# Two attention sublayers of a decoder: one ring of three PSUM bank pairs, exponentials of two heads at a time, and small operations moved from VectorE to GpSimd

## The chip, the cores and the metric

The kernel runs on one core of a Trainium2 chip. The metric is the time of one execution in microseconds (us); several runs are made and the median is taken. A core has five engines, each with its own queue of instructions that it executes in order: TensorE (PE in the rows, its weight loads PEld), VectorE (DVE), ScalarE (ACT), GpSimd (POOL) and SyncE (SP, which issues transfers). They wait for one another through semaphores. TensorE and the others exchange results in PSUM, which has eight banks of 512 float32 columns on 128 partitions; everything else lies in SBUF. TensorE runs at 2.4 GHz or, when the chip grants less, at 1.2 GHz; the granted clock is given as a share of full speed.

## The reference

A decoder of four layers works on x of shape (4, 512, 128). Each of its twelve sublayers computes `x = layernorm(x + f(x))`. Two of them are self attentions with 16 heads of 8 dimensions, and only they are changed:

```python
# layer 1: l1a
q = q * scale                              # q, k, v: (4, 16, 512, 8)
attn = softmax(einsum('bhnd,bmhd->bhnm', q, k))
return einsum('bhnm,bmhd->bnhd', attn, v) @ w_proj.T + b_proj

# layer 3: l3a
attn = where(causal, einsum('bhqd,bhkd->bhqk', q, k) * scale, -inf)
a = clip(attn, -100, 100)
e = exp(a - max(a))
p = e / (sum(e) + 1e-6) + 1e-8
return einsum('bhqk,bhkd->bhqd', p / sum(p), v) @ w_proj.T
```

## The kernel before

`attention16` builds both sublayers, l1a with the full table and l3a with the causal one. The work is cut into 16 groups m = 0 to 15: four batches of four groups of four heads. What is done to a group is cut into units, and a unit has a part on each of several engines:

- J: projections of one batch. Queries and keys are split into three bf16 parts, high (ScalarE), the remainder "left" (VectorE, L674), middle (ScalarE) and low (VectorE, L679), and written to DRAM; SyncE gathers them per group into QS and KS, so that one bf16 matmul gives a float32 score. J 5 copies the values into Va (L685). In l3a VectorE then adds two sums of values, Vsum (L689, L691).
- A: scores of one query tile for two heads, two matmuls into a pair of banks (L515), and the row maxima on VectorE (L701).
- P: the maxima of a group are split into three bf16 parts by four small VectorE operations (L713 to L719), in l3a after a clip (L709).
- T: eight matmuls transpose these parts into a bank pair (L523), and VectorE adds them to QS (L724), so that the next score matmul has the maximum subtracted.
- B: transposed scores of one key tile for one head (L543) and the exponential on ScalarE, 512 columns (L640). In l3a the columns shrink from 512 to 128 with the key tile, and L is the exponential of the lower clip bound (L540, L633).
- X (l3a alone): the clip of one key tile's exponentials of four heads, on VectorE (L729), `e = max(min(e, 1), LB)`, 2048 to 512 columns.
- V: the value matmuls of one or two key tiles (L570, and L567 for the rows under the causal mask), into bank 6; after the last ScalarE copies the bank (L645).
- F: transposes of that copy (L576) and the division by the sum on VectorE (L748 and L750; in l3a L739 to L750).
- C, W, Y, N: once a batch, concatenation, output projection, norm statistics, norm apply and transposes.

What sets the order is a table per sublayer, CAUSAL and FULL, with CAUSAL_BATCH and FULL_BATCH for what is put in once a batch. The tables name units relative to the current group; every engine walks the same list and executes its part of each unit, in order. An engine that waits therefore holds up all that stands behind it in its own queue.

PSUM before: A and T share two bank pairs (banks 0 to 3), B and L two single banks (4 and 5), V has bank 6, the rest bank 7. GpSimd has little to do here: it clears KS and Mp at the start and computes the reciprocal deviation of the norms.

Of the kernel before, what the change touches and what calls it, by code (L numbers as in the profile page):

```python
# [366 lines left out]
def attention16(k, name, w, causal=False):  # L367
# [38 lines left out]
    place = lambda m, kt: HG * ((m * NT + kt) % sets)  # L406

    def body(block, projected, high_made, rest_made, middle_made, low_made, zeroed, v_taken, pair_ready, pair_free, max_split, s_ready, exp_done,
             clipped, pv_done, o_copied, o_turned, ctx_done, c_turned, c_taken, out_ready, steps, normed, turned, v_summed, xt_made,
# [9 lines left out]
        E = k.sb(name + "E", [P, sets * HG, S])  # L419
# [36 lines left out]
        def _(pe):
# [24 lines left out]
            for u in order:  # L481
                kind, m = u[0], u[1]
                g = m % G
                if u in ut:
# [21 lines left out]
                elif kind == "A":  # L506
                    _, _, qt, hp = u
                    if ut[u] == 0:
                        pe.wait_ge(zeroed, 2)
# [15 lines left out]
                elif kind in "BL":  # L525
                    _, _, kt, j = u
                    n = ub[u]
                    if n == 0:
                        for at in (4, 5, 6):
                            if at in users:  # L530
                                emptied(users[at])
                    if n >= 2:
                        pe.wait_ge(exp_done, n - 1)
                    if kt == 0 and j == 0:
                        pe.wait_ge(pair_free, ut[("T", m)] + 1)
                    o = PS[:, 4 + n % 2, :]
                    pp, par = 2 * g + j // 2, j % 2
                    q0 = kt * P if causal else 0
                    if kind == "L":
                        ins = mm(o, k.maxrows[:, par, :], QS[:, pp, :], start=True, stop=True)  # L540
                    else:
                        o = o[:, q0:S]
# [3091 lines left out]
```

## Time and profile before

| | us |
|---|---|
| median of 3 runs | 2062.26 (2058.0 to 2062.41) |
| profiled execution | 2065.93 |
| its span | 2063.8 |
| VectorE busy in the span | 1394.2 |
| TensorE busy | 1671.3 |
| ScalarE busy | 1009.2 |
| GpSimd busy | 414.3 |

The span is the time between the first and the last instruction; the rest of the profiled execution lies around it. Busy sums over the whole span say little here, since twelve sublayers with different limits follow one another. The sublayer l1a lies from about 285 us to 562 us, l3a from 1463 us to 1792 us. Within them the T units (L724, one a group) mark the groups: the distance between two of them is the time of a group. Consecutive VectorE instructions overlap by some 0.08 us in the records, so the cost of one in a row of several is the distance between two starts.

### The profile page before, as it was taken

What the parts mean: (1) busy time and instruction counts of PE and PEld (TensorE: products, weight loads), DVE (VectorE), ACT (ScalarE), POOL (GpSimd) and SP (SyncE); (2) the same over time, 40 slices, a digit from 0 to 9 for tenths busy, and PEclk for the clock granted to TensorE, in tenths of its full rate; (3) what the DMA queues carried; (4) which work ended last, traced back from release to release, by engine and by line L of the source; (5) the groups of instructions that cost most, each with busy time, mean ns of one, the idle gap of its engine ahead of it and who ended that gap; (6) DMA issues with size and microseconds to landing.
All of it is one profiled execution on the core that took longest, in us unless ns stands there. A gap on an engine that the chain in (4) does not pass through costs nothing. (4 is left out here: it accounts for less than half of the span.)

```text
span 2063.8 us, 32418 instructions
## 1 busy us (share of the span) xinstructions
PE 1671.3 (81%) x11422; PEld 990.5 (48%) x11422; DVE 1394.2 (68%) x3239; ACT 1009.2 (49%) x2161; POOL 414.3 (20%) x575
## 2 busy tenths in 40 slices
PE   5779859999878999957789999973587878798692
PEld 3546533333365666645544444531344444365582
DVE  4646678888584777765566767767788889665434
ACT  3336536666523554535355555542245545465362
POOL 1110030000034666541200000001200000100375
PEclk9989869999989999987799999995688999999797
DMA  4100021221046888850000000000211110000213
GB/s 116 41 1 2 1 71 61 63 62 31 1 165 256 333 326 328 324 180 1 1 1 1 1 1 1 1 1 18 71 56 58 32 58 16 1 2 14 94 53 84
DMA packets 71545, 151.09 MB, mean 73 GB/s; under 512 B 9042, under 2 KB 55419, under 8 KB 66299
## 3 DMA queue, kind: packets, MB, share of 16 engines
q1 hardware_dynamic: 61211, 136.25, 19.0%
q0 software_dynamic: 4992, 10.23, 1.6%
q10 hardware_dynamic: 5184, 2.55, 0.5%
q8 instruction: 93, 1.52, 0.3%
q14 instruction: 65, 0.53, 0.1%
HBM read 124.46 MB, written 29.26 MB: 74 GB/s over the span
## 5 line engine op out<-in xcount | busy, mean ns | idle before, releaser
L162 POOL TENSOR_SCALAR rstd<-MV 128x2 f32<-128x2 f32 (+1 forms) x100 | 25.9, 259 | 999.7 <-DVE MV L130 995.0
L640 ACT ACTIVATE l1aE<-PS 128x512 f32<-128x512 f32 x256 | 142.2, 596 | 75.5 <-PE PS L543 72.9
L701 DVE TENSOR_REDUCE l1aM<-PS 128x2 f32<-128x1024 f32 x128 | 150.4, 1218 | 26.2 <-PE PS L515 24.6
L640 ACT ACTIVATE l3aE<-PS 128x512 f32<-128x512 f32 (+3 forms) x256 | 102.7, 439 | 111.7 <-PE PS L545 108.8
L2582 ACT COPY PT<-PS 128x512 f32<-128x512 f32 x128 | 69.2, 589 | 93.5 <-PE PS L2493 93.2
L701 DVE TENSOR_REDUCE l3aM<-PS 128x2 f32<-128x256 f32 (+3 forms) x128 | 100.2, 817 | 15.7 <-PE PS L517 15.5
L2672 DVE TENSOR_REDUCE M<-PS 128x1 f32<-128x589 f32 x128 | 92.5, 764 | 27.0 <-PE PS L2482 26.7
L1713 PE MATMUL PS<-WB,H 128*128 128x512 f32 x234 | 107.4, 595 | 0.0
L2588 ACT ACTIVATE E<-PS,M 128x589 f32<-128x589 f32 x128 | 95.9, 763 | 17.6 <-DVE M L2672 17.5
L543 PE MATMUL PS<-l1aQS,l1aKS 128*128 128x512 bf16 x256 | 90.6, 388 | 8.5 <-ACT l1aE L640 7.0
L729 DVE SCALAR_TENSOR_TENSOR l3aE<-l3aE,l3aLB 128x2048 f32<-128x2048 f32 (+1 forms) x64 | 94.9, 1482 | 2.7 <-ACT l3aE L640 2.7
L515 PE MATMUL PS<-l1aKS,l1aQS 128*128 128x512 bf16 x256 | 82.2, 406 | 16.0 <-DMA l1aKS<-head_image 9.4
L1853 ACT ACTIVATE H<-PS,WB 128x128 f32<-128x128 f32 x156 | 44.6, 368 | 90.8 <-PE PS L1701 90.7
L543 PE MATMUL PS<-l3aQS,l3aKS 128*128 128x512 bf16 (+3 forms) x256 | 76.7, 322 | 10.3 <-ACT l3aE L640 9.7
L2510 PE MATMUL PS<-PT,Va 128*64 128x512 f32 x320 | 82.8, 616 | 0.8 <-ACT Q L2593 0.8
L2493 PEld LDWEIGHTS PS<-cols_const_sb,E 128*128 128x128 f32 x512 | 58.2, 144 | 49.6 <-DVE E L2692 29.4
L515 PE MATMUL PS<-l3aKS,l3aQS 128*128 128x128 bf16 (+3 forms) x256 | 66.9, 316 | 15.1 <-DVE l3aM L701 8.9
L164 POOL TENSOR_TENSOR rstd<-rstd,mhalf 128x2 f32<-128x2 f32 (+1 forms) x100 | 75.9, 759 | 8.3
L2482 PE MATMUL PS<-K,Q 64*128 64x512 f32 x256 | 75.1, 664 | 0.0
L1866 ACT ACTIVATE A<-PS,WB 128x128 f32<-128x128 f32 x156 | 58.7, 457 | 32.4 <-PE PS L1723 32.4
L2493 PE MATMUL PS<-cols_const_sb,E 128*128 128x128 f32 x512 | 71.4, 283 | 2.8 <-DVE E L2692 2.6
L2692 DVE TENSOR_SCALAR E<-E,sums 128x589 f32<-128x589 f32 x128 | 67.6, 528 | 4.5
(671 smaller groups left out, 4273.1 us busy)
## 6 DMA issues: line engine op xcount, KB each, us to landing
WB<-in_experts SPq DMA_DIRECT2D x39, 1286.0 KB
TB<-mixed_tails SPq DMA_DIRECT2D x39, 768.5 KB, 7.1
l1aQS<-head_image SPq DMA_DIRECT2D x16, 256.0 KB, 2.9
l1aKS<-head_image SPq DMA_DIRECT2D x32, 128.0 KB, 3.0
l3aQS<-head_image SPq DMA_DIRECT2D x16, 256.0 KB, 2.9
l3aKS<-head_image SPq DMA_DIRECT2D x32, 128.0 KB, 3.1
head_image<-l1aparts SPq DMA_DIRECT2D x8, 384.0 KB, 2.5
head_image<-l3aparts SPq DMA_DIRECT2D x8, 384.0 KB, 2.5
```

Of the source, the lines that this page charges most:

```text
L164: g.tensor_tensor(out, out, self.mhalf[:, 0:out.shape[1]], ALU.pow).then_inc(done, 1)
L515: ins = mm(o, QS[:, pp, qt * P:(qt + 1) * P], KS[:, pp, par, 0:kc], start=True, stop=not causal)
L543: ins = mm(o, KS[:, pp, par, kt * P:(kt + 1) * P], QS[:, pp, q0:S], start=True, stop=not causal)
L640: nc.scalar.activation(E[:, place(m, kt) + j, q0:S], PS[:, 4 + n % 2, q0:S], ACT.Exp, scale=SCALE).then_inc(exp_done, 1)
L701: v.tensor_reduce(M[:, m % 2, qt, 2 * hp:2 * hp + 2], PS[:, bank:bank + 2, 0:kc], AX, ALU.max, negate=True).then_inc(pair_free, 1)
L729: v.scalar_tensor_tensor(e, e, 1.0, LB[:, m % 2, :, kt * P:S], ALU.min, ALU.max).then_inc(clipped, 1)
L1713: mm(o, H1[:, i % 3, c * P:(c + 1) * P], mid_w(i, c), start=False, stop=False)
L2482: ins = mm(PS[:, at_ + 2 * par, :], Q[own, b % 2, pp, q], K[own, b % 2, pp, :], start=True, stop=True)
L2493: ins = nc.tensor.transpose(PS[:, at_ + 2 * par, t * P:(t + 1) * P], E[:, ring(x, par), e0:e0 + P], k.ident)
L2510: ins = mm(PS[64 * par:64 * par + 64, 6, :], Va[:, b % 2, t, h * DH:(h + 1) * DH], PT[:, n % 2, par, t, :], start=(t == 0), stop=(t == len ...
L2588: nc.scalar.activation(E[:, i, 0:NK], scores(s, par), ACT.Exp, bias=M[:, i:i + 1], accum_out=sums[:, i:i + 1]).then_inc(exp_done, 1)
L2672: ins = v.tensor_reduce(M[:, i:i + 1], scores(s, par), AX, ALU.max, negate=True)
```

## The change

There is now one ring of three bank pairs (banks 0 to 5) through which A, T, B and L go in the order of the table: unit i has pair i modulo 3 and waits until the unit three places ahead has been read. B and L take two heads, so that one exponential reads 1024 columns of two banks. E holds five key tiles instead of three. V is one unit of all four key tiles of a group. In l1a KS has no padded half: each score matmul reads 64 rows, the two heads of a pair in the two row halves, and KS is gathered by one transfer instead of two.

On GpSimd now: P, the low parts of the queries and keys of batches 1 to 3, and the Vsum additions of l3a. The clearing of Va moves from VectorE's start to just ahead of the first value copy. GpSimd walks the table too, the norm operations included.

```diff
-    ('B', 0, 2, 1), ('B', 0, 2, 2), ('V', 0, 0, 1), ('B', 0, 2, 3), ('X', 0, 1), ('B', 0, 3, 0), ('T', 1), ('X', 0, 2), ('B', 0, 3, 1),
+    ('B', 0, 0, 1), ('A', 1, 1, 1), ('B', 0, 1, 1), ('B', 0, 1, 0), ('X', 0, 0), ('A', 2, 0, 0), ('B', 0, 3, 1), ('X', 0, 1), ('P', 1),
+    ('B', 0, 2, 1), ('B', 0, 3, 0), ('B', 0, 2, 0), ('X', 0, 3), ('X', 0, 2), ('T', 1), ('A', 2, 0, 1), ('V', 0, 0, 4),
...
+    ('B', -1, 3, 1), ('T', 0), ('V', -1, 0, 4), ('A', 1, 0, 0), ('B', 0, 1, 0), ('A', 1, 2, 1), ('B', 0, 1, 1), ('A', 1, 1, 1),
...
+    SLOTS, SETS = 3, 5
+    rows_of = lambda par: slice(0, P) if causal else slice(64 * par, 64 * par + 64)
...
+    pairs = [u for u in order if u[0] in "ABLT"]
+    slot_of = {u: i % SLOTS for i, u in enumerate(pairs)}
...
-                    n = ut[u]
-                    bank = 2 * (n % 2)
+                    bank = 2 * slot_of[u]
...
-                        ins = mm(o, QS[:, pp, qt * P:(qt + 1) * P], KS[:, pp, par, 0:kc], start=True, stop=not causal)
+                        own = rows_of(par)
+                        key = KS[:, pp, par, :] if causal else KS[own, pp, :]
+                        ins = mm(o, QS[own, pp, qt * P:(qt + 1) * P], key[:, 0:kc], start=True, stop=not causal)
...
+                elif kind == "P":
+                    pool.wait_ge(pair_free, ut[last_a[m]] + 1)
...
+                    if causal:
+                        step(g.tensor_scalar(Mg, Mg, -LIM, LIM, ALU.max, ALU.min))
+                        step.wait()
+                    maxima, rest = (a.rearrange("p t (a r) -> p a t r", a=2) for a in (Mg, Mleft[:, :, :]))
+                    high, middle, low = (Mp[:, :, :, DK * i + AUG_SLOT:P:64] for i in range(3))
+                    step(g.tensor_copy(high, maxima))
+                    step.wait()
+                    step(g.tensor_tensor(rest, maxima, high, ALU.subtract))
+                    step.wait()
+                    step(g.tensor_copy(middle, rest))
+                    step.wait()
+                    g.tensor_tensor(low, rest, middle, ALU.subtract).then_inc(max_split, 1)
...
-                        nc.scalar.activation(E[:, place(m, kt) + j, q0:S], PS[:, 4 + n % 2, q0:S], ACT.Exp, scale=SCALE).then_inc(exp_done, 1)
+                        q0, at = kt * P if causal else 0, place(m, kt) + 2 * hp
+                        nc.scalar.activation(E[:, at:at + 2, q0:S], PS[:, bank:bank + 2, q0:S], ACT.Exp, scale=SCALE).then_inc(exp_done, 1)
```

The order on TensorE in a plain group of l1a, around the value unit (L570, now L583), before:

```order
L515 MATMUL PS<-l1aKS,l1aQS 128x512 x2
L543 MATMUL PS<-l1aQS,l1aKS 128x512
L570 MATMUL PS<-l1aE,l1aVa 32x512 x8
L515 MATMUL PS<-l1aKS,l1aQS 128x512 x2
L543 MATMUL PS<-l1aQS,l1aKS 128x512 x2
L576 MATMUL PS<-cols_const_sb,l1aOs 128x128 x4
L523 MATMUL PS<-ident_b,l1aMp 128x128 x8
```

and after (L538 is T, L530 A, L554 B):

```order
L538 MATMUL PS<-ident_b,l1aMp 128x128 x8
L583 MATMUL PS<-l1aE,l1aVa 32x512 x16
L530 MATMUL PS<-l1aKS,l1aQS 128x512 x2
L554 MATMUL PS<-l1aQS,l1aKS 128x512 x2
L530 MATMUL PS<-l1aKS,l1aQS 128x512 x2
```

The value work of a group stood in two halves between score matmuls; now it is one block directly behind T's transposes, and the next pair of scores for a maximum stands behind the block.

The order on VectorE in a plain group of l3a, from the clip of the first key tile to T, before:

```order
L701 TENSOR_REDUCE l3aM<-PS 128x2 x3
L729 SCALAR_TENSOR_TENSOR l3aE<-l3aE,l3aLB 128x2048
L709 TENSOR_SCALAR l3aM<-l3aM 128x16
L713 CAST l3aMp<-l3aM 128x16
L715 TENSOR_TENSOR l3aMleft<-l3aM,l3aMp 128x2x4x2
L717 CAST l3aMp<-l3aMleft 128x16
L719 TENSOR_TENSOR l3aMp<-l3aMleft,l3aMp 128x16
L729 SCALAR_TENSOR_TENSOR l3aE<-l3aE,l3aLB 128x4x384
L724 TENSOR_TENSOR l3aQS<-PS,l3aQS 128x1024
```

and after (L745 the maxima, L757 X, L751 T):

```order
L745 TENSOR_REDUCE l3aM<-PS 128x2 x4
L757 SCALAR_TENSOR_TENSOR l3aE<-l3aE,l3aLB 128x2048
L745 TENSOR_REDUCE l3aM<-PS 128x2
L757 SCALAR_TENSOR_TENSOR l3aE<-l3aE,l3aLB 128x4x384
L757 SCALAR_TENSOR_TENSOR l3aE<-l3aE,l3aLB 128x4x128
L757 SCALAR_TENSOR_TENSOR l3aE<-l3aE,l3aLB 128x4x256
L751 TENSOR_TENSOR l3aQS<-PS,l3aQS 128x1024
```

The five splitting operations are gone from VectorE's queue, and all four clips stand ahead of T. The five now stand on GpSimd, whose queue in a plain group of l3a holds only them:

```order
L643 TENSOR_SCALAR l3aM<-l3aM 128x16
L647 CAST l3aMp<-l3aM 128x16
L649 TENSOR_TENSOR l3aMleft<-l3aM,l3aMp 128x2x4x2
L651 CAST l3aMp<-l3aMleft 128x16
L653 TENSOR_TENSOR l3aMp<-l3aMleft,l3aMp 128x16
```

Each of them waits for the one ahead of it, the first for the last maximum of the group. On TensorE in the same group, from T to the next maximum's scores, before:

```order
L570 MATMUL PS<-l3aE,l3aVa 32x512 x4
L543 MATMUL PS<-l3aQS,l3aKS 128x256
L545 MATMUL PS<-causalT_b,ident_b 128x128
L543 MATMUL PS<-l3aQS,l3aKS 128x128
L545 MATMUL PS<-causalT_b,ident_b 128x128
L523 MATMUL PS<-ident_b,l3aMp 128x128 x8
```

and after:

```order
L530 MATMUL PS<-l3aKS,l3aQS 128x128
L532 MATMUL PS<-causal_b,ident_b 128x128
L530 MATMUL PS<-l3aKS,l3aQS 128x128
L532 MATMUL PS<-causal_b,ident_b 128x128
L583 MATMUL PS<-l3aE,l3aVa 32x512 x4
L580 MATMUL PS<-l3aLB,l3aVsum 32x128 x8
L580 MATMUL PS<-l3aLB,l3aVa 32x128 x4
L583 MATMUL PS<-l3aE,l3aVa 32x384 x4
L583 MATMUL PS<-l3aE,l3aVa 32x256 x4
L583 MATMUL PS<-l3aE,l3aVa 32x128 x4
L530 MATMUL PS<-l3aKS,l3aQS 128x384
```

The first value tile stood ahead of T's transposes; now the whole value unit stands behind T and one pair of scores, and the next scores for VectorE behind it.

## Rows read from the trace of the kernel before

**Rows 1.** Stretches: us, busy us of PE, PEld, DVE, ACT, POOL, PEclk, DMA.

```profile
300.00:317.00 17.00, 12.53 (x32) 2.81 (x32) 14.55 (x16) 1.57 (x3) 0.00 (x0) 0.50 0.19 61
1488.00:1764.00 276.00, 226.51 (x2081) 124.44 (x2081) 240.11 (x399) 147.95 (x329) 3.69 (x8) 0.90 0.13 41
```

**Rows 2.** Timeline, VectorE, one group of l3a: start, us, engine, line, [idle before <-releaser].

```profile
1715.28 1.22 DVE L724 TENSOR_TENSOR l3aQS<-PS,l3aQS 128x1024 bf16<-128x1024 f32 x1
...
1719.07 0.42 DVE L701 TENSOR_REDUCE l3aM<-PS 128x2 f32<-128x256 f32 x1 [0.50 <-PE PS L517]
...
1725.91 2.28 DVE L729 SCALAR_TENSOR_TENSOR l3aE<-l3aE,l3aLB 128x2048 f32<-128x2048 f32 x1
1728.11 0.17 DVE L709 TENSOR_SCALAR l3aM<-l3aM 128x16 f32<-128x16 f32 x1
...
1729.11 1.75 DVE L729 SCALAR_TENSOR_TENSOR l3aE<-l3aE,l3aLB 128x1536 f32<-128x1536 f32 x1
1731.94 1.23 DVE L724 TENSOR_TENSOR l3aQS<-PS,l3aQS 128x1024 bf16<-128x1024 f32 x1 [1.08 <-PE PS L523]
```

**Rows 3.** Groups by form, l3a: count | busy us, mean ns | idle before.

```profile
L701 DVE TENSOR_REDUCE l3aM<-PS 128x2 f32<-128x256 f32 x32 | 13.4, 420 | 12.5 <-PE PS L517 12.5
```

**Rows 4.** Timeline, l1a: T units, one wait of VectorE, one value unit.

```profile
311.31 1.23 DVE L724 TENSOR_TENSOR l1aQS<-PS,l1aQS 128x1024 bf16<-128x1024 f32 x1 [1.26 <-PE PS L523]
...
375.49 2.50 DVE L701 TENSOR_REDUCE l1aM<-PS 128x2 f32<-128x1024 f32 x2 [1.48 <-PE PS L515]
...
482.19 1.92 PE L570 MATMUL PS<-l1aE,l1aVa 128*32 128x512 f32 x16
...
507.80 1.22 DVE L724 TENSOR_TENSOR l1aQS<-PS,l1aQS 128x1024 bf16<-128x1024 f32 x1
...
521.33 1.22 DVE L724 TENSOR_TENSOR l1aQS<-PS,l1aQS 128x1024 bf16<-128x1024 f32 x1
...
534.45 1.23 DVE L724 TENSOR_TENSOR l1aQS<-PS,l1aQS 128x1024 bf16<-128x1024 f32 x1
```

**Rows 5.** Timeline, TensorE, l3a: transposes of T, first value tile, lower-bound matmuls.

```profile
1652.89 0.61 PE L523 MATMUL PS<-ident_b,l3aMp 128*128 128x128 bf16 x8
...
1728.44 1.94 PE L570 MATMUL PS<-l3aE,l3aVa 128*32 128x512 f32 x8 [1.27 <-DVE l3aE L729]
...
1730.82 1.01 PE L523 MATMUL PS<-ident_b,l3aMp 128*128 128x128 bf16 x8
...
1731.99 0.65 PE L567 MATMUL PS<-l3aLB,l3aVsum 128*32 128x128 f32 x16
```

**Rows 6.** Groups by form: the maxima of l1a, exponentials of 512 and 1024 columns.

```profile
L701 DVE TENSOR_REDUCE l1aM<-PS 128x2 f32<-128x1024 f32 x128 | 150.4, 1218 | 26.2 <-PE PS L515 24.6
L640 ACT ACTIVATE l1aE<-PS 128x512 f32<-128x512 f32 x256 | 142.2, 596 | 75.5 <-PE PS L543 72.9
L2265 ACT ACTIVATE E<-E 128x1024 f32<-128x1024 f32 x8 | 8.5, 1060 | 10.8 <-DVE E L2301 10.6
```

**Rows 7.** Timeline, VectorE and GpSimd together at three places.

```profile
927.25 1.13 DVE L2065 SCALAR_TENSOR_TENSOR R<-WB,pair_w,R 128x128 f32<-128x128 f32 x4
927.43 0.24 POOL L162 TENSOR_SCALAR rstd<-MV 128x2 f32<-128x2 f32 x1
...
930.75 1.13 DVE L2065 SCALAR_TENSOR_TENSOR R<-WB,pair_w,R 128x128 f32<-128x128 f32 x4
930.90 1.05 POOL L162 TENSOR_SCALAR rstd<-MV 128x2 f32<-128x2 f32 x1
...
1768.28 0.66 DVE L729 SCALAR_TENSOR_TENSOR l3aE<-l3aE,l3aLB 128x512 f32<-128x512 f32 x1
1768.45 0.56 POOL L162 TENSOR_SCALAR rstd<-MV 128x2 f32<-128x2 f32 x1
```

**Rows 8.** Groups by form, GpSimd: count | busy us, mean ns | idle before.

```profile
L1782 POOL TENSOR_TENSOR rs<-rs,mhalf 128x1 f32<-128x1 f32 x78 | 44.0, 564 | 6.5
L2845 POOL TENSOR_TENSOR R<-R,YB 128x512 f32<-128x512 f32 x3 | 3.8, 1256 | 9.1 <-ACT YB L2906 9.1
```

More of the change, by code:

```diff
@@ L390, in attention16 @@
     ut, ub = (count([u for u in order if u[0] in kinds]) for kinds in ("AT", "BL"))
+    pairs = [u for u in order if u[0] in "ABLT"]
+    slot_of = {u: i % SLOTS for i, u in enumerate(pairs)}
+    slot_prev = {u: pairs[i - SLOTS] for i, u in enumerate(pairs) if i >= SLOTS}
     uj = count([u for u in order if u[0] == "J" and u[2] not in (2, 4)])
-    pairs = list(ut)
+    first = lambda kinds: {m: next(u for u in pairs if u[0] in kinds and u[1] == m) for m in range(NG)}
+    first_a, first_b = first("A"), first("BL")
     last_a = {u[1]: u for u in ut if u[0] == "A"}
+    last_b = {u[1]: i for u, i in ub.items() if u[0] == "B"}
+    last_exp = {u[1:3]: i + 1 for u, i in ub.items() if u[0] == "B"}
+    last_low = {u[1]: i + 1 for u, i in ub.items() if u[0] == "L"}
     singles = [u for u in order if u in uj or u[0] in "FCWN"]
-    ring = (7, 4, 5, 6)
+    ring = (7, 6, 5, 4)
     bank_of, bank_prev, users = {}, {}, {}
@@ L418, in body @@
         Mp = k.sb(name + "Mp", [P, 2, NT, P], BF16)
[L419 removed]
+        E = k.sb(name + "E", [P, SETS * HG, S])
         Os = k.sb(name + "Os", [P, 2, S])
@@ L525, in _ @@
                 elif kind in "BL":
[L526 to L542, printed above, removed]
-                        ins = mm(o, KS[:, pp, par, kt * P:(kt + 1) * P], QS[:, pp, q0:S], start=True, stop=not causal)
-                        if causal:
-                            ins = mm(o[:, 0:P], k.ident_b, k.causalT_b, start=False, stop=True)
+                    hp = u[-1]
+                    if u == first_b[m]:
+                        pe.wait_ge(pair_free, ut["T", m] + 1)
+                    pp = 2 * g + hp
+                    for par in range(2):
+                        o = PS[:, bank + par, :]
+                        if kind == "L":
+                            ins = mm(o, k.maxrows[:, par, :], QS[:, pp, :], start=True, stop=True)
+                        else:
+                            kt = u[2]
+                            q0 = kt * P if causal else 0
+                            own = rows_of(par)
+                            key = KS[:, pp, par, :] if causal else KS[own, pp, :]
+                            ins = mm(o[:, q0:S], key[:, kt * P:(kt + 1) * P], QS[own, pp, q0:S], start=True, stop=not causal)
+                            if causal:
+                                ins = mm(o[:, q0:q0 + P], k.ident_b, k.causalT_b, start=False, stop=True)
                     ins.then_inc(s_ready, 1)
@@ L602, in _ @@
             g = nc.gpsimd
-            g.memset(KS[P // 2:P, :, 0, :], 0.0).then_inc(zeroed, 1)
-            pool.wait_ge(zeroed, 1)
-            g.memset(KS[0:P // 2, :, 1, :], 0.0).then_inc(zeroed, 1)
-            pool.wait_ge(zeroed, 2)
             g.memset(Mp[:, :, :, :], 0.0).then_inc(zeroed, 1)
-            for b in range(BT):
-                k.norm_gpsimd(pool, b, b)
+            if causal:
+                pool.wait_ge(zeroed, 1)
+                g.memset(KS[P // 2:P, :, 0, :], 0.0).then_inc(zeroed, 1)
+                pool.wait_ge(zeroed, 2)
+                g.memset(KS[0:P // 2, :, 1, :], 0.0).then_inc(zeroed, 1)
@@ L660, in _ @@
             step = Count(dve, steps)
-            step(v.memset(Va[:, :, :, :, :], 0.0))
-            step.wait()
-            step(v.memset(Va[:, :, :, :, AUG:AUG + 1], 1.0))
             for u in order:
@@ L698, in _ @@
                     dve.wait_ge(pair_ready, ut[u] + 1)
-                    bank = 2 * (ut[u] % 2)
+                    bank = 2 * slot_of[u]
+                    if u == first_a[m] and m >= 2:
+                        dve.wait_ge(max_split, m - 1)
                     kc = (qt + 1) * P if causal else S
@@ L732, in _ @@
                     dve.wait_ge(o_turned, m + 1)
+                    if causal and g == 0:
+                        dve.wait_ge(v_summed, b + 1)
                     turned_o = PS[:, bank_of[u], :].rearrange("p (t j d) -> p t j d", t=NT, j=HG)
```

127 lines of the change are left out of this document (66 added, 61 removed), and 18 rows, old and new, of tables (CAUSAL, CAUSAL_BATCH, FULL, FULL_BATCH).

## The prediction

> **What bounds the kernel now.** The change touches two of twelve sublayers, the full attention l1a and the causal attention l3a, so I read those stretches alone. First the table by stretch [rows 1]: from the first T unit of l3a to the last, 276 us, VectorE is busy 240.1 of 276, ScalarE 148, GpSimd 3.7, and the granted clock is 0.90. VectorE sets the pace there. Then the timeline of VectorE over one plain causal group [rows 2], T to T: 16.66 us. In it VectorE waits twice, 0.50 us for a score pair and 1.08 us for T's transposes, and works the rest. Its five splitting operations (P, L709 to L719) fill 1.00 us, from 1728.11 to 1729.11. The grouped row behind [rows 3] says the same of all groups: the maxima of 256 columns wait 12.5 us in total for TensorE.
>
> In l1a sixteen T units start between 311.31 and 534.45, 223.1 us, and a plain group takes 13.53 [rows 4]. VectorE has one long wait per group there, 1.48 us behind the value and transpose work.
>
> **The change, full attention.** P leaves VectorE: about 0.95 us of work less per group. But the value unit is now one, of four key tiles, straight behind T on TensorE, and the next maximum stands behind both. A unit of two tiles took 1.92 us [rows 4], that is 0.86 a tile and 0.2 of run-in and end; four take 3.45. The cycle that closes on itself is then: transposes 0.6 [rows 5], values 3.45, change of tile form 0.15 (an estimate), a score pair 0.42, seven maxima of 1.2 [rows 6] less 0.04 overlap each, one F of 0.5 (estimate from its two operations), 0.2 for the B pair ahead of T: 13.5 to 13.6. So P's microsecond returns as a wait for V, about 2.4 where 1.48 was. ScalarE, now eight exponentials of 1024 columns, has 8 x 1.06 + 0.6 = 9.1 us [rows 6] of 13.6 and stays behind that; sixteen of 512 cost 9.5. Score matmuls on 64 rows each: 512 columns at 2.4 GHz are 0.21 us, so a pair costs 0.21 if the two row halves run side by side and 0.42 if not (estimates); only one pair a group is on the path. Projections of the next batch no longer stop VectorE as they do (low parts on GpSimd, spread over two groups): about 2.7 us a batch back, 8 in all. Against that stands the clock. With half the score columns, TensorE is lightly used between V and the next T; at the head, where scores alone run beside maxima, it was granted 0.50 for 17 us [rows 1]. I charge 0.5 us a group, 8 in all: nothing left. Head (the 3.5 us memset of Va no longer stands ahead of the first projections) -0.8, tail (eight exponentials, none of them waiting for a single bank) -2. **Full: -3**, from -12 (no clock loss) to +25 (below).
>
> **The change, causal attention.** Without P the 16.66 us group leaves 16.66 - 1.58 - 1.00 = 14.08 of VectorE work. If nothing new waited, the group would take 14.3 to 14.8, and the stage would gain over 30 us. What speaks against this is where P now runs. Its five operations depend on one another, all read SBUF, and they start when the last maximum, A(1,1,1), is done. At that moment VectorE starts X(0,0), then one short maximum, then X(0,1), X(0,3), X(0,2), then T, which needs P. X is a scalar_tensor_tensor with both operands in SBUF.
>
> The trace shows what such an instruction does to a small GpSimd operation [rows 7]. At 1768.28 an X of 512 columns starts; the 0.24 us operation that GpSimd starts at 1768.45 takes 0.56 and ends 0.07 us behind that X. At 930.75 four two-operand VectorE instructions run back to back until 931.88; the GpSimd operation begun at 930.90 takes 1.05 and ends at 931.95, again 0.07 behind the last of them: it was not let in between. In the four that start at 927.25 one did slip in (0.24 at 927.43). So P's first operation is held by X(0,0) until its end; the second fits beside the short maximum; the other three come when the row of X is over. The Trainium skill, "SBUF — State Buffer", section "Who interferes with whom", has the rule: a VectorE instruction with two SBUF inputs and a GpSimd instruction that reads SBUF exclude each other, and whichever issues first holds the shared port for its whole length. By these rows the trace agrees on the exclusion. Read instruction by instruction the rule would let GpSimd in at each border between two X, so that one operation instead of three is left at the end; the sum would then be 10 us lower than mine. The row at 930.90 is the nearer one, and I keep three.
>
> The price, with time 0 at the end of X(0,2). P ends at 0.07 + 2 x (0.08 + 0.25) = 0.73. A GpSimd operation on 128x16 is not in the trace; 0.25 lies by the 0.24 of rows 7, the other bound is the 0.56 of rows 8, which would add 0.9 a group. Hand-over 0.1. T's transposes 0.61 at full clock, 1.01 at half [rows 5]. So VectorE waits 1.44 for T, or 1.84; before it was 1.08. Behind T on TensorE's queue stand A(2,0,1) (0.25) and the whole value unit, 0.86 x (1 + 0.75 + 0.5 + 0.25) = 2.15 and 0.65 for the lower-bound matmuls [rows 5], then the score pair that VectorE needs next (0.45): 3.5 us. VectorE has 1.14 (T) + 0.34 (maximum of 256) to do: it waits 2.0. Before, V lay in four units between the X operations, so this is new. Sum: 14.08 + 1.44 + 2.0 = **17.5 at full clock.**
>
> The clock: while P is held, TensorE has nothing to do for nearly 4 us. Before, 1.27 us without work behind a light stretch (the idle time in the row at 1728.44, [rows 5]) was enough that the first value tile took 1.94 us, twice 0.86 and some, and T 1.01. In the new order T (+0.40), A(2,0,1) (+0.25) and the first value tile (+1.08) come just then: +1.7, so 19.2 in a group where the level falls. I take 19.0.
>
> Fifteen groups of 19.0 are 285. Per batch, beyond that: one q/k remainder 0.75, value copy 0.69 and its 0.29 on VectorE, projections and the concat transposes on TensorE about 1.1, norm apply 1.1, about 4; the norm statistics fall into the wait for V. Three batches: 12. First to last T: 297 for 276, **+21**. The low parts (1.26 us each on GpSimd [rows 8]) and the value sums run beside maxima of other groups, which read PSUM, and nobody waits for them. Head -0.5; tail (the last X waited for exponentials of single heads) -3. **Causal: +17.5.**
>
> The profiled execution took 2065.93, 3.7 above the median of the runs. 2065.9 - 3 + 17.5 = 2080.4 there, 2077 as a median.
>
> **Rivals.** (A) *P is ready in time.* If X does not hold these operations, or GpSimd gets in ahead of X(0,0), P ends 1.7 us after A(1,1,1) and VectorE reaches T 6 us after it. Then TensorE does T and half of V below the X, the wait for V is 0.3 to 0.7, a group takes 14.8 and a batch 7 extra: 222 + 20 = 242 for 276, -34. With head, tail and the full stage: **2022**. For it: the load row of [rows 2]. Against: every row of [rows 7]. It decides from the point at which three of P's five operations are through before X(0,1) starts. Chance 0.20.
> (B) *P is held but the clock stays up*, or GpSimd gets in at borders: 17.5 x 15 + 12 = 274.5, -1.5; total -8, **2054**. For it: T at 1652.89 ran in 0.61 [rows 5]. Chance 0.17.
> (C) *The full stage pays too.* Its A/B stretch leaves TensorE at half speed until well into V: T +0.3, pair +0.2, half of V's 3.45 doubled +1.7 = 2.2 a group, 33 in all, 25 more than I charge: **2102** with the causal loss. For it: 0.50 at the head [rows 1]. Against: V and F lie in between and keep TensorE busy. Chance 0.10.
> (D) *The full stage gains.* If the three-pair ring lets scores run far enough ahead that V is covered, a group takes VectorE's work, 11.1 to 12: -1.7 x 15 = -25, **2052** with the causal loss. Against: the first maximum behind V stands behind it in TensorE's queue. Chance 0.08.
>
> **How the numbers follow.** The forecast (P held, clock down in most groups, 2066 to 2095) has 0.45; (A) to (D) 0.20, 0.17, 0.10, 0.08. A measurement of this kernel can tell about 0.2%, 4 us, from no change. Faster than 2058: A, D, most of B: 0.38. Within: the rest of B, the low end of the forecast: 0.09. Slower than 2066: 0.53. Of the range, 2030 at the low end leaves out part of A (0.12) and 2098 most of C (0.07).
>
> **What will show it.** Right: in l3a GpSimd operations of P that take 0.5 to 2 us instead of 0.25 and end together with an X; VectorE idle 1.4 to 1.9 before T and about 2 before the first maximum behind V; T starts 18 to 20 us apart; T's eight matmuls at 1.0. In l1a T starts 13.5 to 14.2 apart with one wait of about 2.4, P on GpSimd at its plain price (no VectorE instruction there has two SBUF operands). Wrong: P's five operations in l3a end within 2 us of the last maximum, T starts 14.5 to 15 apart: then A. Wrong in the full stage: a granted clock under 0.9 there, or no wait behind V.

## The result, and the profile after

The changed kernel takes 2076.43 us (median of 20 runs, 2065.05 to 2086.04), the kernel before 2060.97 (20 runs, 2056.34 to 2066.46): 1.007 times as long, 95% interval 1.0058 to 1.0082. The forecast was 2077 within 2030 to 2098, and slower. The profiled execution has a span of 2076.0 us.

Where the time went is read from the two sublayers apart. From its first projection to the start of the next sublayer (its first matmul behind l1a, its first VectorE instruction behind l3a), l1a takes 268.1 us instead of 277.1, l3a 351.0 instead of 331.8; the rest of the difference between the two spans, 2.0 us, lies outside both. So a gain of 9.0 stands against a loss of 19.2.

The stretches of the changed kernel from the first T to the last, l1a and l3a (columns as in [rows 1]):

```profile
312.00:530.00 218.00, 178.03 (x1206) 61.28 (x1208) 178.76 (x215) 139.34 (x153) 27.97 (x78) 0.91 0.16 52
1478.00:1774.00 296.00, 225.62 (x2063) 131.92 (x2077) 223.80 (x319) 129.81 (x181) 103.31 (x95) 0.87 0.12 38
```

The second row answers to the second of [rows 1]. VectorE has 16.3 us less to do (240.1 before, 223.8 now): P's five operations were 15.0 us there and the low parts and the value sums 8.2, and some of it comes back as X that last longer and as X and F that moved into the stretch. But it stands idle for 72 us where it stood for 36. GpSimd is busy for 103 us where it was for 4. The groups by form say which waits these are and who is busy:

```profile
L745 DVE TENSOR_REDUCE l3aM<-PS 128x2 f32<-128x768 f32 x32 | 30.4, 951 | 46.0 <-PE PS L532 46.0
L751 DVE TENSOR_TENSOR l3aQS<-PS,l3aQS 128x1024 bf16<-128x1024 f32 x16 | 19.5, 1221 | 23.7 <-PE PS L538 23.7
L643 POOL TENSOR_SCALAR l3aM<-l3aM 128x16 f32<-128x16 f32 x16 | 31.9, 1997 | 150.6 <-DVE l3aM L745 150.6
...
L647 POOL CAST l3aMp<-l3aM 128x16 bf16<-128x16 f32 x16 | 13.0, 815 | 1.1
L649 POOL TENSOR_TENSOR l3aMleft<-l3aM,l3aMp 128x16 f32<-128x16 f32 x16 | 19.0, 1189 | 1.4
L651 POOL CAST l3aMp<-l3aMleft 128x16 bf16<-128x16 f32 x16 | 7.0, 435 | 1.0
L653 POOL TENSOR_TENSOR l3aMp<-l3aMleft,l3aMp 128x16 bf16<-128x16 f32 x16 | 9.1, 571 | 1.3
```

The first maximum behind the value block waits 46.0 us in all, T 23.7 (2.8 of it ahead of the first group). The five GpSimd operations of P take 2.00, 0.82, 1.19, 0.44 and 0.57 us on the mean. The same four without the clip take 0.26, 0.24, 0.25 and 0.27 in l1a (L647 to L653). One group of l3a, VectorE and GpSimd, shows why:

```profile
1604.88 2.28 DVE L757 SCALAR_TENSOR_TENSOR l3aE<-l3aE,l3aLB 128x2048 f32<-128x2048 f32 x1
1607.08 0.41 DVE L745 TENSOR_REDUCE l3aM<-PS 128x2 f32<-128x256 f32 x1
1607.41 3.52 DVE L757 SCALAR_TENSOR_TENSOR l3aE<-l3aE,l3aLB 128x1536 f32<-128x1536 f32 x3
1612.33 1.22 DVE L751 TENSOR_TENSOR l3aQS<-PS,l3aQS 128x1024 bf16<-128x1024 f32 x1 [1.39 <-PE PS L538]
...
1605.05 2.23 POOL L643 TENSOR_SCALAR l3aM<-l3aM 128x16 f32<-128x16 f32 x1 [12.63 <-DVE l3aM L745]
1607.35 0.26 POOL L647 CAST l3aMp<-l3aM 128x16 bf16<-128x16 f32 x1
1607.69 1.57 POOL L649 TENSOR_TENSOR l3aMleft<-l3aM,l3aMp 128x16 f32<-128x16 f32 x1
1609.32 0.59 POOL L651 CAST l3aMp<-l3aMleft 128x16 bf16<-128x16 f32 x1
1609.99 1.07 POOL L653 TENSOR_TENSOR l3aMp<-l3aMleft,l3aMp 128x16 bf16<-128x16 f32 x1
```

The clip of P starts 0.17 us after X(0,0) and ends at 1607.28, 0.12 behind it. The next operation falls beside the maximum, which reads PSUM, and takes 0.26. The other three each last until one of the three X in the row at 1607.41 is over; the last ends at 1611.06, 0.13 behind the end of that row. TensorE, at half clock (granted 0.50) after 2.9 us without work, does T from 1611.21 in 1.01 us:

```profile
1608.06 0.22 PE L556 MATMUL PS<-causalT_b,ident_b 128*128 128x128 bf16 x1
1611.21 1.01 PE L538 MATMUL PS<-ident_b,l3aMp 128*128 128x128 bf16 x8 [2.93 <-POOL l3aMp L653]
```

Not every group goes this way. In six of the fifteen behind the first T, P ends 0.13 us behind the last X and T waits 1.40, as here. In two, the second operation does not get in at either border between the three X, takes 3.65 us, and leaves three operations for the time behind the X; T then waits 2.37:

```profile
1627.90 3.48 DVE L757 SCALAR_TENSOR_TENSOR l3aE<-l3aE,l3aLB 128x1536 f32<-128x1536 f32 x3
1633.75 1.22 DVE L751 TENSOR_TENSOR l3aQS<-PS,l3aQS 128x1024 bf16<-128x1024 f32 x1 [2.37 <-PE PS L538]
...
1627.85 3.65 POOL L647 CAST l3aMp<-l3aM 128x16 bf16<-128x16 f32 x1
```

In three groups a value sum on GpSimd, held by X(0,0), delays P's first operation (T waits 2.04); in three a projection's VectorE instruction stands between the X and P is done before the last of them (no wait); the last group, whose A(2,0,0) is missing, waits 1.73. The last plain group of all shows the two waits and the first value tile:

```profile
1755.46 1.22 DVE L751 TENSOR_TENSOR l3aQS<-PS,l3aQS 128x1024 bf16<-128x1024 f32 x1 [1.40 <-PE PS L538]
1760.12 1.56 DVE L745 TENSOR_REDUCE l3aM<-PS 128x2 f32<-128x768 f32 x2 [3.10 <-PE PS L532]
...
1755.71 1.88 PE L583 MATMUL PS<-l3aE,l3aVa 128*32 128x512 f32 x8
```

### The profile page after: what moved, and what is told of

Read it like the earlier page. It is cut to its first block and busy times, and to the rows that moved or that the text cites. A ratio compares the mean times of both kernels' runs of the same rounds, so it can differ in the third digit from the quotient of the medians.

```text
span 2076.0 us, 32345 instructions
## 1 busy us (share of the span) xinstructions
PE 1635.2 (79%) x11384; PEld 986.3 (48%) x11422; DVE 1354.6 (65%) x3075; ACT 974.9 (47%) x1873; POOL 534.3 (26%) x737
## 3 DMA queue, kind: packets, MB, share of 16 engines
q1 hardware_dynamic: 60955, 136.25, 18.6%
## 5 line engine op out<-in xcount | busy, mean ns | idle before, releaser
L745 DVE TENSOR_REDUCE l1aM<-PS 128x2 f32<-128x1024 f32 x128 | 148.6, 1217 | 34.3 <-PE PS L530 34.1
L162 POOL TENSOR_SCALAR rstd<-MV 128x2 f32<-128x2 f32 (+1 forms) x100 | 25.6, 256 | 502.3 <-DVE MV L130 498.1
L687 ACT ACTIVATE l1aE<-PS 128x1024 f32<-128x1024 f32 x128 | 129.0, 1026 | 21.5 <-PE PS L554 16.8
L745 DVE TENSOR_REDUCE l3aM<-PS 128x2 f32<-128x256 f32 (+3 forms) x128 | 99.5, 815 | 47.4 <-PE PS L532 47.1
L687 ACT ACTIVATE l3aE<-PS 128x1024 f32<-128x1024 f32 (+3 forms) x128 | 84.8, 708 | 36.1 <-PE PS L556 34.0
L757 DVE SCALAR_TENSOR_TENSOR l3aE<-l3aE,l3aLB 128x2048 f32<-128x2048 f32 (+1 forms) x64 | 95.0, 1519 | 1.0 <-ACT l3aE L687 1.0
L554 PE MATMUL PS<-l1aQS,l1aKS 64*128 64x512 bf16 x256 | 54.2, 423 | 38.1 <-DVE l1aM L745 33.0
L554 PE MATMUL PS<-l3aQS,l3aKS 128*128 128x128 bf16 (+2 forms) x255 | 60.2, 303 | 19.0 <-DVE l3aM L745 12.5
L530 PE MATMUL PS<-l3aKS,l3aQS 128*128 128x384 bf16 (+3 forms) x255 | 67.1, 319 | 8.6 <-DVE l3aM L745 6.9
L643 POOL TENSOR_SCALAR l3aM<-l3aM 128x16 f32<-128x16 f32 x16 | 31.9, 1997 | 150.6 <-DVE l3aM L745 150.6
```

The costliest lines, as they stand in the source:

```text
L554: ins = mm(o[:, q0:S], key[:, kt * P:(kt + 1) * P], QS[own, pp, q0:S], start=True, stop=not causal)
L687: nc.scalar.activation(E[:, at:at + 2, q0:S], PS[:, bank:bank + 2, q0:S], ACT.Exp, scale=SCALE).then_inc(exp_done, 1)
L745: v.tensor_reduce(M[:, m % 2, qt, 2 * hp:2 * hp + 2], PS[:, bank:bank + 2, 0:kc], AX, ALU.max, negate=True).then_inc(pair_free, 1)
L757: v.scalar_tensor_tensor(e, e, 1.0, LB[:, m % 2, :, kt * P:S], ALU.min, ALU.max).then_inc(clipped, 1)
```

## The experiments

Each kernel is the changed one with the edit that is named. The table has what all their traces give: us from the first projection of a sublayer to the next sublayer, and between its first and last T. Each ratio is to runs of the kernel before that were made beside it (medians 2057.6 to 2062.3), with its 95% interval.

| kernel | time | ratio to before | l1a | l3a | l3a, T to T |
|---|---|---|---|---|---|
| before | 2061 | | 277.1 | 331.8 | 276.0 |
| changed | 2076.4 | 1.007 (1.006 to 1.008) | 268.1 | 351.0 | 295.9 |
| e1, X with one operand | 2006.4 | 0.976 (0.971 to 0.980) | 267.4 | 284.0 | 232.0 |
| e2, P on VectorE behind X(0,1) | 2054.1 | 0.998 (0.996 to 1.001) | 267.4 | 333.9 | 280.0 |
| e3, l3a as before | 2051.5 | 0.997 (0.994 to 0.999) | 267.9 | 327.9 | 272.2 |
| e4, all X behind T | 2032.5 | 0.989 (0.984 to 0.993) | 267.8 | 311.6 | 252.8 |
| e5, P on VectorE ahead of X(0,0) | 2042.9 | 0.989 (0.985 to 0.994) | 268.3 | 320.0 | 268.3 |
| e6, values behind three maxima | 2084.6 | 1.012 (1.009 to 1.015) | 268.1 | 357.2 | 302.2 |
| e7, l1a with P on VectorE | 2089.7 | 1.016 (1.011 to 1.020) | 284.1 | 351.1 | 296.1 |
| e8, l1a with padded keys | 2071.7 | 1.006 (1.004 to 1.009) | 270.7 | 347.3 | 292.1 |
| e9, P ahead of the X on GpSimd | 2031.5 | 0.986 (0.985 to 0.988) | 267.3 | 310.2 | 258.9 |
| e10, the same, shorter gap | 2032.2 | 0.985 (0.981 to 0.989) | 268.1 | 306.3 | 255.1 |
| e11, e9 with units respaced | 2027.1 | 0.985 (0.981 to 0.989) | 269.6 | 304.5 | 253.6 |

Stage lengths come from one execution each; the same l3a before stands at 331.8 in one and at 327.9 in e3's, so differences of 4 us say little.

**e1: the second SBUF operand of X taken away.**

```diff
-                    v.scalar_tensor_tensor(e, e, 1.0, LB[:, m % 2, :, kt * P:S], ALU.min, ALU.max).then_inc(clipped, 1)
+                    v.tensor_reduce(e, e.unsqueeze(3), AX, ALU.max).then_inc(clipped, 1)
```

> The changed kernel with one edit in the causal sublayer: X reads one SBUF operand instead of two (a maximum over an axis of length one, in place, over the same elements). The clip itself is left out, its place, length and waits stay. Theory HOLD (two-operand X instructions hold P's five operations on GpSimd): P's operations in l3a fall from 2.0, 0.8, 1.2, 0.4, 0.6 us to about 0.25 each as in l1a, the wait of 1.4 us before T goes, TensorE does T and half of V below the X, T starts 14.5 to 15.5 apart; first to last T 296 -> 240 to 255, the kernel 2076 -> about 2030. Theory ORDER (the value unit in one block behind T, with TensorE at half clock, costs this whatever P does): P short, but T starts still 18 or more apart, the kernel within 8 us of 2076.

Measured: 2006.4 us, l3a 67 us shorter. X kept its length, P lost its waits, and so did VectorE:

```profile
L757 DVE TENSOR_REDUCE l3aE<-l3aE 128x2048 f32<-128x2048 f32 x16 | 36.4, 2273 | 1.0 <-ACT l3aE L687 1.0
L643 POOL TENSOR_SCALAR l3aM<-l3aM 128x16 f32<-128x16 f32 x16 | 4.2, 265 | 140.6 <-DVE l3aM L745 140.6
L745 DVE TENSOR_REDUCE l3aM<-PS 128x2 f32<-128x768 f32 x32 | 30.3, 949 | 9.9 <-PE PS L532 9.3
...
1471.00:1704.00 233.00, 201.58 (x2113) 121.33 (x2130) 219.43 (x320) 129.87 (x181) 37.51 (x95) 0.98 0.16 49
```

The X of 2048 columns takes 2.27 us for 2.28, the clip of P 0.27 for 2.00, and the wait behind the block falls from 46.0 to 9.9 us. The last row is the stretch from first to last T: the granted clock is 0.98 where it was 0.87, so in l3a the half clock was a consequence of the late P, not a cause of its own. The order of all units is that of the changed kernel, which settles HOLD against ORDER. The gain was larger than expected (T to T 232 for 240 to 255; the kernel 2006 for about 2030). The edit frees the value sums and the low parts on GpSimd as well, so not every microsecond of it need be P's.

**e2 and e5: P on VectorE, late and early.**

```diff
+P_VECTOR = lambda causal: causal
...
-                elif kind == "P":
+                elif kind == "P" and not P_VECTOR(causal):
...
+                elif kind == "P" and P_VECTOR(causal):
...
```

The second cut is in GpSimd's part, the third in VectorE's, where the same five operations follow.

> The changed kernel with one edit in the causal sublayer: the five operations of P go back to VectorE, at the place that P has in the new table (between X(0,1) and X(0,3)). HOLD: VectorE has 1.0 us more work a group, no wait before T; T starts 15.3 to 16 apart, first to last T 296 -> 250 to 260, the kernel about 2033. ORDER: T starts 18 or more apart, the kernel 2068 or more.

Measured: 2054.1, between the two. The wait before T is gone, but not the one behind the block. This is one plain group of e2: P's last operation, the two X behind it, T, and the first three maxima, the last two in one row:

```profile
1733.88 0.23 DVE L768 TENSOR_TENSOR l3aMp<-l3aMleft,l3aMp 128x16 bf16<-128x16 f32 x1
1733.98 1.82 DVE L779 SCALAR_TENSOR_TENSOR l3aE<-l3aE,l3aLB 128x512 f32<-128x512 f32 x2
1735.72 1.21 DVE L773 TENSOR_TENSOR l3aQS<-PS,l3aQS 128x1024 bf16<-128x1024 f32 x1
1736.85 0.41 DVE L748 TENSOR_REDUCE l3aM<-PS 128x2 f32<-128x256 f32 x1
1740.23 1.55 DVE L748 TENSOR_REDUCE l3aM<-PS 128x2 f32<-128x768 f32 x2 [2.97 <-PE PS L535]
```

P ends at 1734.1, 5.3 us behind the start of the clips (X(0,0) at 1728.79), because its place in the table is behind X(0,1). I had overlooked that the engine is not all: P is late there on VectorE too, T and the block start late, and the block costs its 3 us. e5 moves P ahead of X(0,0).

```diff
-    ('B', 0, 0, 1), ('A', 1, 1, 1), ('B', 0, 1, 1), ('B', 0, 1, 0), ('X', 0, 0), ('A', 2, 0, 0), ('B', 0, 3, 1), ('X', 0, 1), ('P', 1),
+    ('B', 0, 0, 1), ('A', 1, 1, 1), ('P', 1), ('B', 0, 1, 1), ('B', 0, 1, 0), ('X', 0, 0), ('A', 2, 0, 0), ('B', 0, 3, 1), ('X', 0, 1),
```

> As the run with P on VectorE in the causal sublayer, but P stands directly behind the last maximum, ahead of X(0,0), instead of behind X(0,1). That run lost the wait before T (1.3 us in all) but kept a wait of 3 us behind the value block, since P still ended late and T and the block with it. LATE (what costs is that P ends late, on whichever engine): here P ends 1 us behind the last maximum, TensorE does T and half of the block below the X, the wait behind the block falls from 36 us in all to under 12; T starts 15.0 to 16.2 apart, first to last T 296 -> 242 to 258, the kernel 2018 to 2036. BLOCK (the one value unit costs its 3 us wherever P ends): the kernel 2048 to 2058 as with P behind X(0,1).

Measured: 2042.9. The wait behind the block falls from 36.1 us in all to 19.0, more than LATE's bound of 12, and the time lies between the two ranges. What is left of the wait is seen on TensorE. P ends at 1708.98 there, but T stands in TensorE's queue behind score pairs that wait 1.60 us for a bank, which the maximum behind X(0,0) frees. T then ran at 1712.09, 2.7 us ahead of VectorE's T, and yet the first value tile met the half clock:

```profile
1711.53 0.23 PE L557 MATMUL PS<-l3aQS,l3aKS 128*128 128x128 bf16 x1 [1.60 <-DVE l3aM L748]
...
1712.09 0.66 PE L541 MATMUL PS<-ident_b,l3aMp 128*128 128x128 bf16 x8
...
1713.11 1.94 PE L586 MATMUL PS<-l3aE,l3aVa 128*32 128x512 f32 x8
1714.82 1.08 PE L583 MATMUL PS<-l3aLB,l3aVsum 128*32 128x128 f32 x16
```

Only one other group has so long a first tile (1.94); T itself took about 1.06 in five. Why e1, in nearly the same order, stays close to full clock is not shown. Against e1, VectorE has 21 us more work from first to last T here (240.55 in 269 us for 219.43 in 233) and 15 us more idle time. The work is P's: 15 us, and 6 more because in three groups its clip and its first copy, 0.17 and 0.20 us elsewhere, took 1.1 to 1.2 while GpSimd worked on the low parts or a value sum. So ending P early is one part of the matter and VectorE's saved microsecond another; of the kernels tried, those with P on GpSimd and no hold have both.

**e6: the value block moved away from T.** `('V', -1, 0, 4)` stands behind the first three score pairs of the next group, and F behind it; P stays under the X. The two L units move as well: they stood between those score pairs and now stand behind the block.

> P stays on GpSimd under the X as in the changed kernel; only the value unit of the causal sublayer moves, behind the first three score pairs of the next group, and F with it. This prices the second part of the loss alone. P's operations stay long and the wait before T stays at 1.0 to 1.4 us; the wait behind the block (47 us in all) falls to under 20. First to last T 296 -> 258 to 275, the kernel 2040 to 2058. If the wait behind the block is not what the late P costs, under 8 us change.

Measured: 2084.6, a miss. The wait did not shrink; it moved from the second maximum behind T to the fifth:

```profile
1721.02 1.23 DVE L751 TENSOR_TENSOR l3aQS<-PS,l3aQS 128x1024 bf16<-128x1024 f32 x1 [2.37 <-PE PS L538]
1722.16 3.09 DVE L745 TENSOR_REDUCE l3aM<-PS 128x2 f32<-128x256 f32 x4
1728.48 1.23 DVE L745 TENSOR_REDUCE l3aM<-PS 128x2 f32<-128x1024 f32 x1 [3.23 <-PE PS L532]
```

The block then starts at 1723.91 instead of right behind T, and the maxima that stand ahead of it were to cover it with 3.1 us of work that the late T had also delayed; the two L units now lie between the block and the next pair, 0.9 us more. Taken alone, a change of 8 us in the wrong direction speaks rather for the second reading that was named. It is e1 that ties the wait to the late P; e6 shows that moving the block alone does not buy it back.

**e3, e7, e8: the full sublayer.** e3 builds l1a with the changed function and l3a with the function of before.

> The change in the full sublayer alone: l1a as changed, l3a as before. By the two traces l1a takes 268.1 instead of 277.1 from its first projection to the next sublayer, so the kernel should take 2061 - 9 = 2052 (2046 to 2057), both theories alike. If it takes 2061 or more, the nine microseconds were no gain of that sublayer.

Measured: 2051.5, as expected, with l1a at 267.9. Against the runs beside it, at 2057.6, that is 0.3% (0.1 to 0.6), so the time alone says only that the sublayer gains; the nine microseconds rest on the stage lengths. e7 gives l1a's P back to VectorE, behind the maximum of A(1,3,0).

> The changed kernel with P of the full sublayer back on VectorE, behind the maximum of A(1,3,0), so that it ends 5 us before T. In l1a no VectorE instruction reads two SBUF operands, so this is what the move is worth where nothing holds it. If VectorE sets the cycle, 0.95 us a group: 16 x 0.95 = 15, l1a 268 -> 283, the kernel 2091 (2086 to 2097). If, as the prediction's sum has it, the microsecond returns as a shorter wait behind the value block, within 5 us of 2076.

Measured: l1a 284.1 for 268.1, the kernel 2089.7. The move of P is worth 16.0 us where nothing holds it, about 0.95 us in each of 16 groups; the prediction had let it return as a wait. Not all of it is P's work, though: in six more groups than in the changed kernel TensorE did T in 1.03 us instead of 0.62, and the maxima behind the block waited 2 us longer in all. e8 pads the keys again, so that a pair's two matmuls take the whole array one after the other.

> The changed kernel with the keys of the full sublayer padded to 128 rows again, so that the two heads of a pair follow one another on TensorE instead of side by side: a pair costs 0.43 instead of 0.23 us. The prediction charged 0.5 us a group for a clock that falls because TensorE has too little to do. If that is so, the granted clock of the stage rises from 0.91 to 0.97 or more and the longer pairs cost little: l1a 264 to 271. If the clock was not what a group waited for, the one pair on the path costs 0.2 us a group and the second transfer of keys a little: l1a 270 to 276, the kernel 2077 to 2084.

Measured: l1a 270.7, and the granted clock of its stretch rises from 0.91 to 0.99:

```profile
309.00:527.00 218.00, 202.03 (x1193) 73.05 (x1190) 180.33 (x212) 136.82 (x150) 27.51 (x77) 0.99 0.16 51
```

The 270.7 lies in both ranges, and the kernel's 2071.7 below the second theory's 2077 to 2084, so the times do not separate the two. The clock rose as the first had it, and the stage still ended 2.6 us later. What the half clock costs is read better from the changed kernel itself, from T's transposes and the value block, on which VectorE waits in l1a:

```profile
429.63 0.62 PE L538 MATMUL PS<-ident_b,l1aMp 128*128 128x128 bf16 x8
430.18 3.64 PE L583 MATMUL PS<-l1aE,l1aVa 128*32 128x512 f32 x32
```

In 14 of the 15 groups behind the first T they take 0.62 and 3.64 us, as in e8, at a granted clock of 1.00; in the other, 1.03 and 3.89. The low clock of the stage falls into other stretches, and on this path it costs 0.7 us in all.

**e4, e9, e10, e11: P on GpSimd, clear of the X.** Only the causal table and its batch units differ. In e4 T, too, stands ahead of all X, and the value block behind three score pairs; in e9 to e11 the X keep their place ahead of T, and F and one or two short maxima move between the last maximum and X(0,0), so that GpSimd has the 1.6 us that P takes. This is the middle of e9's edit:

```diff
-    ('B', 0, 0, 1), ('A', 1, 1, 1), ('B', 0, 1, 1), ('B', 0, 1, 0), ('X', 0, 0), ('A', 2, 0, 0), ('B', 0, 3, 1), ('X', 0, 1), ('P', 1),
+    ('B', 0, 0, 1), ('A', 1, 1, 1), ('P', 1), ('B', 0, 1, 1), ('F', -1), ('B', 0, 1, 0), ('A', 2, 0, 0), ('A', 2, 0, 1), ('X', 0, 0),
```

> The changed kernel with another causal table and nothing else: P stays on GpSimd, but between the last maximum and T VectorE now has F and two short maxima, and all four X stand behind T; the value unit stands behind three score pairs of the next group. HOLD: P's operations about 0.25 us each, a wait of 0.5 us or less before T, TensorE's block of values covered by three maxima; VectorE 14.1 of work and 1.0 to 1.6 of waits, T starts 15.0 to 16.0 apart, first to last T 240 to 258, the kernel 2025 to 2040. ORDER: the block of values is covered too, so this run alone does not tell the theories apart; it shows what the move of P to GpSimd is worth where nothing holds it.

> The changed kernel with another causal table: P stays on GpSimd, all X and T keep their order and the value unit its place behind T, but F and the two maxima A(2,0,0) and A(2,0,1) move between the last maximum and X(0,0), about 2.0 us of VectorE work. HOLD: P's operations take about 0.25 to 0.35 each and end 1.7 to 2.0 us behind the last maximum, TensorE does T and most of the block below the X as in the run with one-operand clips, granted clock 0.95 or more; plain T starts 13.8 to 14.8 apart, first to last T 296 -> 230 to 245, l3a from its first projection to the next sublayer 351 -> 284 to 298, the kernel 2008 to 2024: faster than both kernels by 2%. If the gain of the one-operand run came from something else than the hold, the stage stays above 320.

Measured: e4 2032.5, e9 2031.5. In both P's operations take 0.24 to 0.33 us on the mean; one group of e9:

```profile
1719.06 0.26 POOL L643 TENSOR_SCALAR l3aM<-l3aM 128x16 f32<-128x16 f32 x1 [14.46 <-DVE l3aM L745]
1719.38 0.26 POOL L647 CAST l3aMp<-l3aM 128x16 bf16<-128x16 f32 x1
1719.72 0.24 POOL L649 TENSOR_TENSOR l3aMleft<-l3aM,l3aMp 128x16 f32<-128x16 f32 x1
1720.03 0.26 POOL L651 CAST l3aMp<-l3aMleft 128x16 bf16<-128x16 f32 x1
1720.37 0.27 POOL L653 TENSOR_TENSOR l3aMp<-l3aMleft,l3aMp 128x16 bf16<-128x16 f32 x1
...
1712.64 1.56 DVE L745 TENSOR_REDUCE l3aM<-PS 128x2 f32<-128x768 f32 x2 [0.35 <-PE PS L532]
1714.99 3.91 DVE L745 TENSOR_REDUCE l3aM<-PS 128x2 f32<-128x1024 f32 x4 [0.80 <-PE PS L532]
```

e4 lies inside its range. e9 misses its own by 8 us: plain T starts are 16.0 apart instead of 13.8 to 14.8, because without F between them the maxima wait for score pairs whose banks L still holds (0.80 above), and the batch projections cost 4 us more than in e1. Two more tables were tried on that.

> As the run before it, with F and one maximum (1.65 us) between the last maximum and X(0,0), the last maximum being A(1,2,0) of 768 columns, and A(2,0,1) behind T. P's chain of 5 x 0.25 + 4 x 0.08 = 1.6 us just fits; if F's two-operand instructions or X(0,0) catch its last operation, that one is held for up to 2.3 us, and TensorE has T 2 us later but still below the X. Within 8 us of the run before it (2005 to 2028).

> As the run with the split ahead of the clips (2031 us, plain groups of 16.0, groups with projections of 20.4), with the waits that its trace shows taken on: L stands behind the second and the fourth score pair instead of ahead of them (VectorE waited 0.80 us for a pair whose banks L held), and the projections J 1 and J 5 stand between the X, where TensorE has room, instead of ahead of the value block (2.87 us) and among the maxima (0.99 us). Plain T starts 15.0 to 15.8, groups with projections 17 to 18.5; l3a 297 to 305, the kernel 2012 to 2026. If the waits only move, within 5 us of 2031.

Measured: 2032.2 and 2027.1. e10 lies above its range, though within 8 us of e9; P's second, third and last operation took 0.32 to 0.38 on the mean there, and X(0,0) 2.47 for 2.28. e11's plain groups take 15.5 and l3a 304.5, both as expected, and its stretch from first to last T keeps a granted clock of 0.99; but its time is 1 us above its range and also within the 5 us that were to mean that the waits only move. It is the fastest of the kernels that compute all of it, by 1.5% against before (interval 1.1 to 1.9); whether it is faster than e9 is not settled by four runs each. e1's 284.0 us for l3a remain the mark that a table without the hold could reach. Why these stop 20 us short is seen only in part: waits for L's banks, batch units, and in e11 the hold in the other direction, of VectorE by GpSimd:

```profile
L757 DVE SCALAR_TENSOR_TENSOR l3aE<-l3aE,l3aLB 128x1024 f32<-128x1024 f32 x16 | 22.7, 1416 | 0.0
L757 DVE SCALAR_TENSOR_TENSOR l3aE<-l3aE,l3aLB 128x512 f32<-128x512 f32 x16 | 16.5, 1031 | 0.0
```

In e9 the same X take 1216 and 682 ns. Nine X of e11, three a batch, run beside low parts or value sums on GpSimd and take about 1 us longer each, 9 us in all.

## Why the prediction was right

- *P under the X is held.* Right, and the two-operand X is its cause, by e1. The step read it from rows of an operation (L162) that has nothing to do with P [rows 7], as no trace had P on GpSimd yet.
- *Three operations are left when the X are over.* Right in two groups, wrong in most. In six, GpSimd was let in at each border between two X, and P ended 0.13 us behind the last, not 0.73. In two it was not let in at either border, and the three operations stood behind the X as predicted; there P ended 1.10 behind them. Both rows of [rows 7] thus have their like here, and what decides at a border is not shown. By its instruction-by-instruction reading, the Trainium skill ("SBUF — State Buffer", section "Who interferes with whom": whoever issues first holds the pair for the whole instruction) gave the first case, and the trace agrees with it in those six groups. It does not agree in the two: the cast at 1627.85 starts 0.05 us ahead of X(0,1) in the records and yet waits for all three X. T's wait was 1.40 us on the mean of the fifteen groups, for 1.84.
- *TensorE goes to half clock and T and the first value tile pay.* Right in most groups: T took 1.01 in twelve of fifteen, the first tile 1.88 to 1.94 in ten. The wait behind the block was 3.10 in the last plain group, for 2.0 + 0.25 + 1.08 = 3.3.
- *The value sums run beside maxima, and nobody waits for them.* Wrong in three groups. The second sum was held by X(0,0) and took 3.36 us, X(0,1) behind it 2.48 to 2.49 for 1.75, and P's first operation started only when the sum was done, so that T waited 2.04.
- *19.0 a plain group, +21 from first to last T.* Measured 18.6 to 20.1, and +19.9. Two errors went against each other: T waited less than predicted, so that a group without batch units took 18.6, and the batch units cost 17 in all for 12. The tail was to gain 3 and lost 0.4; the head gained 1.0 for 0.5. l3a: +19.2 for +17.5.
- *l1a gains 3.* It gained 9.0. From first to last T it gained 5.6, where the sum had nothing left. The step that failed is the clock charge of 0.5 us a group, 8 in all: T and the value block ran at full clock in 14 of 15 groups, and the half clock cost 0.7 us there. The block itself took 3.64 for 3.45. The sentence that P's microsecond returns as a wait for V was wrong in what it compared. In the changed order the wait is there (2.06 at 434.18, for 2.4 expected), but e7 shows that with P on VectorE it stays (31.5 us over all groups for 29.3) and P comes on top.

```profile
434.18 6.88 DVE L745 TENSOR_REDUCE l1aM<-PS 128x2 f32<-128x1024 f32 x6 [2.06 <-PE PS L530]
```

- The sum, 2077, hit 2076.4 partly by luck. It had +14.5 us for the two sublayers; the traces show +10.2, since l1a was put 6 us too high and l3a 1.7 too low. The medians differ by 15.5, the profiled executions by 12.0, of which 2 lie outside the two sublayers.
- *Rival A* fell with P's rows; no row of [rows 2] speaks for it. e1 shows what it would have been: 2006, lower than the 2022 worked out, as l3a's first to last T took 232 for 242 and l1a gained 9.7 for 3.
- *Rival B* named two conditions. GpSimd did get in at borders in most groups, but T and the first tile ran at half clock all the same, and a group took 18.6 instead of B's 17.5. *C* fell with the full clock of T and the block in l1a. *D* had VectorE's work alone set a group of l1a; the wait behind the block, 2.06 in the row above, is what it left out.

## What to carry to other kernels

Before a small operation is moved to GpSimd, look at what VectorE runs beside it: here four VectorE instructions with two SBUF operands, 0.7 to 2.3 us each, turned a chain of five 0.25 us steps into 6 us, and the same move beside PSUM reads was worth its full microsecond per group. Look the other way as well: what is put on GpSimd can hold VectorE, 9 us in e11. A late small step costs more than its own wait when a block of TensorE work stands behind it: in a plain group the wait before T was 1.4 us, the one behind the block 3 us, and the half clock that TensorE met after 2.9 us without work is part of both. And a table of units that puts such a step in a gap of its own is worth trying before giving the engine up: here it turned +0.7% into -1.5%.

## What the runs showed of the hardware that was not expected

The hold works the other way round as well. In e2, where P is not on GpSimd, a sum of values (3.36 us from 1502.46, itself held by the X at 1502.42) was still running when the next X came, and that X, 1.75 us elsewhere, took 2.48. P's clip, now on VectorE and with one SBUF operand, was held too, by the low part on GpSimd: 1.12 us for 0.17, ending 0.03 behind it. So on VectorE it is not two-operand instructions alone that meet the hold, though e1's maximum over one SBUF operand did not:

```profile
1502.42 2.28 DVE L779 SCALAR_TENSOR_TENSOR l3aE<-l3aE,l3aLB 128x2048 f32<-128x2048 f32 x1
...
1504.96 2.48 DVE L779 SCALAR_TENSOR_TENSOR l3aE<-l3aE,l3aLB 128x1536 f32<-128x1536 f32 x1
1507.37 1.12 DVE L758 TENSOR_SCALAR l3aM<-l3aM 128x16 f32<-128x16 f32 x1
...
1502.46 3.36 POOL L638 TENSOR_TENSOR l3aVsum<-l3aVa,l3aVsum 128x512 f32<-128x512 f32 x1
1505.79 2.66 POOL L632 TENSOR_TENSOR l3aparts<-l3aleft,l3aparts 128x512 bf16<-128x512 f32 x1
```

And a GpSimd operation of 128x16 elements, 0.24 to 0.27 us where nothing holds it, is not much slower than the same one on VectorE (0.17 to 0.23 in the kernel before): the chain of five takes 1.6 us there for 1.0.
